# Causal scores in quadrants of 32 queries, and a re-ordered cross-attention stage, in a gated transformer layer on one core

## The chip, the cores and the metric

The kernel runs on one core of a Trainium2 chip. The metric is the device time of one launch in microseconds (us); lower is better. The engines are TensorE (PE, with its weight load PEld shown apart), VectorE (DVE), ScalarE (ACT), GpSimd (POOL) and SyncE (SP), which issues nearly all transfers.

## The reference

The input is 16 sequences of 64 tokens with 256 features. With `ln` for a layer norm and `rms` for an RMS norm, the layer computes:

```
x = x + tanh(g0) * cross(ln(x), ctx)      # reference groups tokens as 2 x 512 queries
x = x + tanh(g1) * ffn(ln(x))
cross: q = x Wq, k = ctx Wk, v = ctx Wv, 16 heads of 128; q, k = rms(q), rms(k) with gains
       softmax(q k^T / sqrt(128)) v, then Wo
ffn:   h = rms(x); causal self-attention over each sequence of 64, 16 heads of 128, then wo
       t = rms(x + attention); router softmax over 16 experts, top 6, weights renormalised
       out = x + attention + sum_e cw_e * down_e(silu(gate_e t) * up_e t) + shared expert
```

In `ffn` the scores of a key later than the query are masked out before the softmax. Everything is float32.

## The kernel before

**Stages.** The 1,024 tokens are two halves of 512. There are six stages in this order: `a` (cross-attention) for half 0 and half 1, `b` (self-attention) for each half, `m` (experts in 25 chunks of 128 hidden units) for each half. `a` and `b` work on pairs of heads: eight pairs a stage, 16 of each kind in all. Every engine's program is one list of calls for each pair or chunk (`cross_pair`, `self_pair`, `chunk`), and semaphores order the engines against each other. The order of calls within each function is written by hand, and an engine never overtakes in it.

**Large products.** Weights and tokens are split into a rounded part `_hi` and a rest `_lo`, and each large product is three float32r matmuls (`project` L538, `add_output` L565, `project_values` L651). DVE and ACT write the `_hi` parts, POOL the `_lo` parts (L1645). Scores, head values and norm sums are plain float32, of which each matmul leaves two records in the trace.

**A cross-attention pair.** For pair `u`, PE runs `norm_q` (L672), `scores` (L697), the value product of the pair before (`context_values`, L729), the next pair's keys 0, queries 0, keys 1, the output of the pair before for head 0, queries 1, the output for head 1, in half 0 `value_out` (L661), and last `norm_k` (L680), the key norm sums of the next pair. Keys 0 of the next pair go to `bank_s`, so they wait until DVE has read the scores from there (semaphore `raw`, L1365). `norm_q` waits until DVE has taken queries 0 from `bank_q` (`qt`, L1407), and `scores` until ACT has taken queries 1 (`qt_1`, L1005). `norm_k` writes `bank_p`. ACT takes keys 0 and squares them, takes keys 1 (L1010), takes the exponentials (L1046), and squares keys 1, queries 0 and queries 1 (L1002). DVE scales the scores, takes and subtracts the maximum, waits for the exponentials, normalises (L1389 to L1393), takes queries 0, transposes the weights (L1401), rounds the weights of the pair after next (L1419) and, in half 0, splits the value product (L1457, `vo_lo`).

**Pieces.** The norms of the next stage's tokens are cut into pieces and put beside pairs and chunks by `plan_of`, each with a pair number and a slot. On DVE in a cross pair slot 2 lies between the subtraction of the maximum and `normalise`, slot 0 in the middle, slot 1 at the end. A "turn" piece transposes tokens on PE into `bank_t` and `bank_p`; `norm_k` of that pair waits until DVE has read them (`release(held)`).

**A self-attention pair.** `scores` (L707) multiplies, for each head and sequence, 64 queries by 64 keys: 16 matmuls of 64 stationary columns and 64 moving ones, two sequences side by side. DVE multiplies by the scale and adds the mask, a row of 64 keys for each query (L1374). PE transposes the normalised weights (`turn_attn`, L714), ACT copies them to `rows_t` (`take_turned`), and `head_values` (L746) uses them.

**Passage to self-attention.** Beside the last cross pair, PE makes the first self-attention pair's queries 0, keys 0, both outputs, queries 1, the last context values, keys 1, values of the first tiles, values of the second tiles. Keys 0 and keys 1 both use `bank_k`; the context values of the last pair use `bank_v`, `bank_s`, `bank_p`, `bank_t`; both halves of the values use `bank_v`, and ACT empties it between them (L1022).

## Time and profile before

| what | value |
|---|---|
| median of 3 runs | 637.55 us (637.42 to 637.81) |
| profiled execution, own time | 637.76 us |
| its span, first to last instruction | 636.0 us |
| outside the span | 1.76 us |
| busy PE / DVE / ACT / POOL | 623.6 / 463.0 / 320.5 / 252.8 us |
| HBM read and written | 48.22 and 1.05 MB |

Busy time is the union of an engine's instructions. PE's instructions overlap each other, so a group's share of the order of work is told by its start and the start of what follows, not by the sum of durations.

### The profile page before, as it was taken

The numbers are of one execution on the slowest core, as the hardware profiler recorded it, in microseconds if no ns is written. First come the engines' busy times: TensorE is split into PE (matmuls) and PEld (weight loads), VectorE is DVE, ScalarE is ACT, GpSimd is POOL, SyncE is SP. The second block draws the span as 40 slices with busy tenths as digits, with TensorE's granted clock in tenths as the row PEclk, the third lists the DMA queues.
The fourth block names the chain that finished last, engine by engine and source line by source line (L and its number), as shares of the span: only waits on it lengthen the run. The fifth ranks groups of instructions, "written<-read, shape, count | busy, mean of one in ns | idle before, by whom it ended". The sixth has DMA issues, their size and how long they took to land.

```text
span 636.0 us, 17180 instructions
## 1 busy us (share of the span) xinstructions
PE 623.6 (98%) x6688; PEld 544.8 (86%) x6688; DVE 463.0 (73%) x913; ACT 320.5 (50%) x699; POOL 252.8 (40%) x336
## 2 busy tenths in 40 slices
PE   8899999999999999999999999999999999999997
PEld 6688888877788998999999998988888888888886
DVE  5878877998886776876677788655556987555556
ACT  6777767677743335333344333354476444444443
POOL 3221121212132533444352444445554665555453
PEclk9999999999999999999999999999999999999999
DMA  7523131111011322222221331113323232333332
GB/s 225 189 64 89 51 97 33 33 46 37 17 51 34 116 73 81 69 67 68 68 87 48 108 91 39 35 51 99 88 87 98 78 101 84 92 97 99 94 90 90
DMA packets 36019, 50.24 MB, mean 79 GB/s; under 512 B 4080, under 2 KB 23024, under 8 KB 35952
## 3 DMA queue, kind: packets, MB, share of 16 engines
q1 hardware_dynamic: 35376, 48.81, 26.1%
q8 instruction: 49, 0.80, 0.5%
q10 hardware_dynamic: 576, 0.48, 0.2%
q14 instruction: 18, 0.15, 0.1%
HBM read 48.22 MB, written 1.05 MB: 77 GB/s over the span
## 4 chain that ended last, share of the span: by engine, by line
PE 88%; DVE 5%; ACT 3%; issue 1%; DMA 1%; SPq 0%; POOL 0%; DVEq 0%; ACTq 0%
PE acc L565 23%; PE bank_q L538 16%; PE bank_k L538 14%; PE bank_s L538 7%; PE bank_v L538 7%; PE bank_v L651 7%; PE bank_s L707 3%; PE bank_p L746 2%; PE bank_s L697 2%; PE bank_k L729 2%; PE bank_t L714 1%; PE bank_k L661 1%; PE bank_p L680 1%; PE bank_q L672 1%; DMA xt<-in_ctx_t 1%
## 5 line engine op out<-in xcount | busy, mean ns | idle before, releaser
L565 PE MATMUL acc<-wo_hi,pv_hi 128*128 128x256 f32 x328 | 93.4, 285 | 0.3 <-DVE pv_lo L1482 0.2
L565 PE MATMUL acc<-wo_lo,pv_hi 128*128 128x256 f32 x328 | 92.9, 283 | 0.0
L565 PE MATMUL acc<-wo_hi,pv_lo 128*128 128x256 f32 x328 | 92.1, 281 | 0.0
L1645 POOL TENSOR_TENSOR wq_lo<-raw_a,wq_hi 128x256 fp32r<-128x256 f32 x32 | 23.6, 738 | 121.2 <-DVE wq_hi L1419 121.2
L565 PEld LDWEIGHTS acc<-wo_hi,pv_hi 128*128 128x128 f32 x328 | 61.5, 188 | 4.9 <-issue 1.8
L1645 POOL TENSOR_TENSOR wq_lo<-raw_m,wq_hi 128x256 fp32r<-128x256 f32 x50 | 40.4, 808 | 60.5 <-DVE wq_hi L1438 59.0
L565 PEld LDWEIGHTS acc<-wo_lo,pv_hi 128*128 128x128 f32 x328 | 61.7, 188 | 2.3
L565 PEld LDWEIGHTS acc<-wo_hi,pv_lo 128*128 128x128 f32 x328 | 62.3, 190 | 0.0
L1482 DVE TENSOR_TENSOR pv_lo<-raw_a,pv_hi 128x512 fp32r<-128x512 f32 (+1 forms) x51 | 37.9, 745 | 33.3 <-ACT pv_hi L1086 33.0
L538 PE MATMUL bank_q<-xt_hi,wq_hi 128*128 128x512 f32 x144 | 59.9, 416 | 0.5 <-POOL wq_lo L1645 0.5
L1086 ACT ACTIVATE pv_hi<-raw_a 128x512 fp32r<-128x512 f32 (+1 forms) x51 | 31.7, 624 | 56.5 <-DVE raw_a L1477 50.8
L1469 DVE TENSOR_TENSOR r_k<-ln_k,unit_w 128x512 f32<-128x512 f32 x44 | 32.0, 727 | 35.4 <-ACT ln_k L1077 35.4
L538 PE MATMUL bank_q<-xt_hi,wq_lo 128*128 128x512 f32 x144 | 56.7, 394 | 0.0
L538 PE MATMUL bank_q<-xt_lo,wq_hi 128*128 128x512 f32 x144 | 56.4, 392 | 0.0
L1645 POOL TENSOR_TENSOR wk_lo<-raw_m,wk_hi 128x256 fp32r<-128x256 f32 x50 | 39.3, 786 | 32.6 <-ACT wk_hi L1161 32.4
L1645 POOL TENSOR_TENSOR wv_lo<-raw_v,wv_hi 128x512 fp32r<-128x512 f32 x16 | 20.6, 1288 | 73.4 <-DVE wv_hi L1445 73.4
L1010 ACT ACTIVATE kt<-bank_k 128x512 f32<-128x512 f32 x48 | 28.7, 598 | 40.7 <-PE bank_k L538 40.6
L538 PE MATMUL bank_k<-xt_hi,wk_hi 128*128 128x512 f32 x114 | 44.9, 394 | 0.2 <-DVE pv_lo L1337 0.2
L538 PE MATMUL bank_k<-xt_lo,wk_hi 128*128 128x512 f32 x114 | 44.9, 394 | 0.0
L538 PE MATMUL bank_k<-xt_hi,wk_lo 128*128 128x512 f32 x114 | 44.6, 391 | 0.0
L1645 POOL TENSOR_TENSOR wq_lo<-raw_b,wq_hi 128x256 fp32r<-128x256 f32 x32 | 24.8, 777 | 48.6 <-DVE wq_hi L1422 48.6
L1645 POOL TENSOR_TENSOR wo_lo<-raw_m,wo_hi 128x256 fp32r<-128x256 f32 x50 | 41.3, 826 | 6.8 <-ACT wo_hi L1155 6.8
(235 smaller groups left out, 1951.6 us busy)
## 6 DMA issues: line engine op xcount, KB each, us to landing
raw_m<-in_chunk_m SPq DMA_DIRECT2D x50, 256.0 KB, 2.7
raw_a<-in_head_a SPq DMA_DIRECT2D x48, 192.0 KB, 3.1
raw_b<-in_head_b SPq DMA_DIRECT2D x32, 256.0 KB, 3.3
raw_m<-in_chunk_m SPq DMA_DIRECT2D x50, 128.0 KB, 2.1
raw_v<-in_pair_v SPq DMA_DIRECT2D x16, 256.0 KB, 3.1
raw_b<-in_head_b SPq DMA_DIRECT2D x32, 128.0 KB, 2.1
xs<-in_x SPq DMA_DIRECT2D x6, 128.0 KB, 3.3
out<-xs SPq DMA_DIRECT2D x3, 256.0 KB, 2.4
```

The lines of the kernel that those rows point to most:

```text
L538: last = nc.tensor.matmul(bank[:], w[:, cols], m(k), start=n == 0, stop=n == 3 * chunks - 1)
L565: last = nc.tensor.matmul(acc[t // 2][:, (t % 2) * D:(t % 2 + 1) * D], w[:, tok], m, start=begins and n == 0, stop=True, skip_group_check= ...
L651: last = nc.tensor.matmul(bank_v[:, b * PAIR:(b + 1) * PAIR], m, w[:, cols], start=n == 0, stop=n == 3 * KD - 1)
L697: last = nc.tensor.matmul(bank_s[j * GROUP:(j + 1) * GROUP, g * SEQ:(g + 1) * SEQ], qt[:, h, queries], kt[:, h, at:at + SEQ], start=True, ...
L707: last = nc.tensor.matmul(bank_s[s * SEQ:(s + 1) * SEQ, g * SEQ:(g + 1) * SEQ], qt[:, h, tok], kt[:, h, tok], start=True, stop=True)
L729: last = nc.tensor.matmul(context_of(u, j)[:, :, n, :], ctx_sb[rows, at:at + C], turned[rows, n, k], start=k == 0, stop=k == 1)
L746: last = nc.tensor.matmul(value_bank(r)[c * SEQ:(c + 1) * SEQ, cols], values[rows, n, width], turned[rows, cols], start=True, stop=True)
L1010: nc.scalar.activation(kt[:, h], bank[:], ACT.Copy).then_inc(stage["kt"], 1)
L1086: nc.scalar.activation(pv_hi[:, u.parity, part], hh[:, part], ACT.Copy).then_inc(M["hh_hi"], 1)
L1469: nc.vector.tensor_tensor(gu, gs, weights, ALU.mult).then_inc(M["weighted"], 1)
L1482: nc.vector.tensor_tensor(pv_lo[:, u.parity, part], hh[:, part], pv_hi[:, u.parity, part], ALU.subtract)\
L1645: nc.gpsimd.tensor_tensor(lo, raw, hi, ALU.subtract).then_inc(signal, 1)
```

## The change

The scores of self-attention are made in quadrants of 32 queries. `g` now stands for (part, head, parity of the sequence), where part 0 is queries 0 to 31 and part 1 is queries 32 to 63. Part 0 is multiplied by keys 0 to 31 alone, part 1 by all 64. That is 32 matmuls of 32 stationary columns, half with 32 and half with 64 moving columns. The quarter of the score tile that is left out is set to -1e30 once (`mask_rest`), and the scaling becomes two DVE instructions. The copy to `rows_t` and the moving operand of `head_values` follow the new order.

In cross-attention: the keys of the first two pairs change banks, so that the first pair need not wait for `raw` before keys 0; `norm_k` writes `bank_v` after a turn and always waits for `qt_1`; the wait for turned tokens moves to the next pair's context values; ACT squares queries 0 before it takes keys 1; DVE takes queries 0 before the slot 2 piece and `normalise`; the pieces `norm` (half 0), `refine` with `centre`, and `refine_root` with `apply` move to slot 2. In the passage to self-attention the first values go before the last context values, and keys 0 and 1 use `bank_s` and `bank_q`. In the expert stage `refine_root` and `apply` run before `split_hidden`.

```diff
-    beside_pairs("a", 0, ("x", 1), stats=(pairs - 5, 2), norm=(pairs - 4, 1), turn=(pairs - 3, 0))
-    beside_pairs("a", 1, ("y", 0), stats=(1, 2), rough=(1, 1), refine=(2, 2), centre=(2, 1), sums=(3, 0), root=(3, 1),
-                 refine_root=(4, 2), apply=(4, 1), turn=(5, 0))
+    beside_pairs("a", 0, ("x", 1), stats=(pairs - 5, 2), norm=(pairs - 4, 2), turn=(pairs - 3, 0))
+    beside_pairs("a", 1, ("y", 0), stats=(1, 2), rough=(1, 1), norm=(2, 2), sums=(3, 0), root=(3, 1), scale=(4, 2),
+                 turn=(5, 0))
...
-            return ((bank_k, bank_p, bank_t, bank_v) if u.deferred else (bank_v, bank_s, bank_p, bank_t))[j]
+            return (bank_k, bank_p, bank_t, bank_v if u.deferred else bank_s)[j]
...
-            return (bank_s, bank_k)[h] if u.kind == "a" else bank_k
+            if u.kind == "a":
+                return (bank_k, bank_s)[h] if u.n <= 2 else (bank_s, bank_k)[h]
+            return (bank_s, bank_q)[h] if u.very_first else bank_k
+        def key_sums(u):
+            turned = u.n > 1 and plan.piece(u.prev())[0] == "turn"
+            return (bank_v if turned else bank_p)[:, 0:HT // 2]
...
             def norm_k(u):
                 pe.wait_ge(A["sq_k"], u.of(1))
+                if not u.very_first:
+                    pe.wait_ge(A["qt_1"], u.n)
...
-                for h in range(2):
-                    for b in range(NS):
-                        t, s = b // SPB, b % SPB
-                        at = sequence_at(t, s) * SEQ
-                        tok = slice(at, at + SEQ)
-                        g = h * NT + t
-                        last = nc.tensor.matmul(bank_s[s * SEQ:(s + 1) * SEQ, g * SEQ:(g + 1) * SEQ], qt[:, h, tok],
-                                                kt[:, h, tok], start=True, stop=True)
+                for g in range(G):
+                    part, h, n = g // 4, g // 2 % 2, g % 2
+                    seen = (part + 1) * GROUP
+                    for j in range(QUADS):
+                        at = (2 * j + n) * SEQ
+                        queries = slice(at + part * GROUP, at + (part + 1) * GROUP)
+                        last = nc.tensor.matmul(bank_s[j * GROUP:(j + 1) * GROUP, g * SEQ:g * SEQ + seen], qt[:, h, queries],
+                                                kt[:, h, at:at + seen], start=True, stop=True)
...
             def cross_pair(u):          # PE
+                    release(turned_tokens(prev))
                     context_values(prev)
                 if nxt.kind == "a":
-                    pe.wait_ge(A["raw"], u.n)
+                    if prev:
+                        pe.wait_ge(A["raw"], u.n)
                     project_keys(nxt, 0)
...
-                if prev:
+                if nxt.kind == "b" or not prev:
+                    pe.wait_ge(A["raw"], u.n)
+                else:
                     pe.wait_ge(A["pv_lo"], QUADS * (prev.n - 1) + 1)
                 project_keys(nxt, int(nxt.kind == "a"))
...
                     project_queries(nxt, 1)
+                    project_values(nxt, False)
+                    pe.wait_ge(B["kt"], nxt.of(0))
                     context_values(u)
                     project_keys(nxt, 1)
-                    pe.wait_ge(A["pv_lo"], QUADS * (u.n - 1) + 2)
-                    project_values(nxt, False)
                     project_values(nxt, True)
+                    pe.wait_ge(A["pv_lo"], QUADS * u.n)
...
             def cross_pair(u):          # ACT
                     square_k(nxt, 0)
+                    square_q(nxt, 0)
                     take_k(nxt, 1)
                 exponentials(u)
                 if nxt.kind == "a":
                     square_k(nxt, 1)
-                    square_q(nxt, 0)
...
                 else:
+                    take_v(nxt, False)
                     take_context_values(u)
                     take_k(nxt, 1)
-                    take_v(nxt, False)
...
+            def mask_rest():
+                v.wait_ge(ld_rest, 16)
+                rest = by_part(sc[:])[:, 0, :, GROUP:SEQ]
+                mask = sm[:, SM_MASK:SM_MASK + GROUP].unsqueeze(1).to_broadcast([P, G // 2, GROUP])
+                link(nc.vector.tensor_scalar(rest, mask, 0.0, -1e30, ALU.mult, ALU.add))
...
-                    nc.vector.scalar_tensor_tensor(sc[:], found, SCALE, mask, ALU.mult, ALU.add).then_inc(B["scaled"], 1)
+                    for part in range(2):
+                        seen = (part + 1) * GROUP
+                        mask = sm[:, SM_MASK + SEQ - seen:SM_MASK + SEQ].unsqueeze(1).to_broadcast([P, G // 2, seen])
+                        scaled = nc.vector.scalar_tensor_tensor(by_part(sc[:])[:, part, :, 0:seen],
+                                                                by_part(found)[:, part, :, 0:seen], SCALE, mask,
+                                                                ALU.mult, ALU.add)
...
             def cross_pair(u):          # DVE
+                if nxt.kind == "a":
+                    take_q(nxt, 0)
                 prepare_piece(*piece_at(u, 2), u)
                 normalise(u)
-                if nxt.kind == "a":
-                    take_q(nxt, 0)
...
-                prepare_piece(*piece_at(u, 1), u)
...
-                with_scalar = piece_at(u)[0] in ("turn", "logits", "spread", "refine_root", "apply")
+                with_scalar = piece_at(u)[0] in ("turn", "logits", "spread")
```

## Rows read from the trace of the kernel before

**Rows 1.** The page: span, busy time by engine, granted clock in 40 slices.
```profile
span 636.0 us, 17180 instructions
...
PE 623.6 (98%) x6688; PEld 544.8 (86%) x6688; DVE 463.0 (73%) x913; ACT 320.5 (50%) x699; POOL 252.8 (40%) x336
...
PEclk9999999999999999999999999999999999999999
```

**Rows 2.** The page: the chain that ended last, by engine.
```profile
PE 88%; DVE 5%; ACT 3%; issue 1%; DMA 1%; SPq 0%; POOL 0%; DVEq 0%; ACTq 0%
```

**Rows 3.** PE's waits over the span: total, times, longest.
```profile
PE bank_s L538 <- DVE sc_sub L1365: 3.0, 4, 0.9
...
PE bank_q L672 <- DVE qt L1407: 0.8, 1, 0.8
PE bank_v L651 <- ACT vs L1022: 0.8, 1, 0.8
...
PE bank_k L729 <- issue: 0.6, 1, 0.6
PE bank_q L538 <- POOL wq_lo L1645: 0.5, 1, 0.5
PE bank_p L680 <- DVE xt_lo L1297: 0.5, 1, 0.5
...
PE bank_k L538 <- DVE pv_lo L1337: 0.2, 1, 0.2
```

**Rows 4.** Timeline, PE: one set each of small matmuls; start, duration.
```profile
208.68 1.15 PE L707 MATMUL bank_s<-kt,qt 128*64 128x64 f32 x32
...
169.29 1.10 PE L697 MATMUL bank_s<-kt,qt 128*32 128x64 f32 x64
...
358.20 0.74 PE L772 MATMUL bank_s<-sm,xt 128*32 128x16 f32 x64
```

**Rows 5.** Groups by form, PE: busy, mean ns of one, idle before.
```profile
L729 PE MATMUL bank_p<-rows_t,ctx_sb 32*128 32x128 f32 x128 | 18.5, 283 | 0.0
...
L714 PE MATMUL bank_t<-sm,attn 128*128 128x128 f32 x64 | 9.7, 274 | 0.0
```

**Rows 6.** PE's waits, 12 to 30 us.
```profile
PE bank_s L538 <- DVE sc_sub L1365: 1.4, 2, 0.9
```

**Rows 7.** Timeline, ACT, first pair.
```profile
21.23 0.59 ACT L1002 ACTIVATE sq_q<-bank_q 128x512 f32<-128x512 f32 x1
...
22.38 0.69 ACT L1005 ACTIVATE qt<-bank_v,gqk 128x512 f32<-128x512 f32 x1
```

**Rows 8.** Timeline, DVE and POOL, around the norm pieces.
```profile
6.05 1.13 DVE L1267 TENSOR_SCALAR hn<-xs,mv 128x256 f32<-128x256 f32 x4
...
67.22 2.51 DVE L1267 TENSOR_SCALAR hn<-xs,mv 128x256 f32<-128x256 f32 x4
...
133.91 2.53 DVE L1277 TENSOR_SCALAR ys<-xs,mv,st 128x256 f32<-128x256 f32 x4
...
133.87 0.73 POOL L1645 TENSOR_TENSOR wq_lo<-raw_a,wq_hi 128x256 fp32r<-128x256 f32 x1 [7.09 <-DVE wq_hi L1419]
...
141.88 0.69 DVE L1389 TENSOR_REDUCE ex_sum<-ex 128x8 f32<-128x512 f32 x1 [0.83 <-ACT ex L1046]
```

**Rows 9.** Timeline, ACT and PE: queries 1 taken in two pairs, one set of norm sums.
```profile
145.59 0.68 ACT L1005 ACTIVATE qt<-bank_v,gqk 128x512 f32<-128x512 f32 x1
...
167.08 0.68 ACT L1005 ACTIVATE qt<-bank_v,gqk 128x512 f32<-128x512 f32 x1
...
168.86 0.64 PE L672 MATMUL bank_q<-sq_q,ones_of 128*32 128x256 f32 x8
```

**Rows 10.** Timeline, DVE and POOL, the expert chunk with `refine_root`.
```profile
472.61 0.69 DVE L1482 TENSOR_TENSOR pv_lo<-raw_a,pv_hi 128x512 fp32r<-128x512 f32 x1 [0.76 <-ACT pv_hi L1086]
...
474.22 0.29 DVE L1438 CAST wq_hi<-raw_m 128x256 fp32r<-128x256 f32 x1
...
474.59 1.11 POOL L1645 TENSOR_TENSOR wq_lo<-raw_m,wq_hi 128x256 fp32r<-128x256 f32 x1 [2.06 <-DVE wq_hi L1438]
```

More of the change, by code:

```diff
@@ L627, in project_keys @@
                 pe.wait_ge(stage["wk_lo"], u.of(h))
-                if h and u.kind == "b":
+                if h and bank is bank_k and u.kind == "b":
                     pe.wait_ge(B["kt"], u.of(0))
+                if h and bank is bank_q:
+                    pe.wait_ge(B["qt"], u.of(1))
                 if u.kind == "a":
@@ L678, in norm_k @@
                 pe.wait_ge(A["sq_k"], u.of(1))
+                if not u.very_first:
+                    pe.wait_ge(A["qt_1"], u.n)
                 for j in range(QUADS):
-                    last = nc.tensor.matmul(bank_p[j * GROUP:(j + 1) * GROUP, 0:HT // 2], ones_of[:, 0:GROUP],
+                    last = nc.tensor.matmul(key_sums(u)[j * GROUP:(j + 1) * GROUP], ones_of[:, 0:GROUP],
                                             quads(sq_k[:])[:, :, :, j, :], start=True, stop=True)
@@ L736, in head_values @@
                 pe.wait_ge(B["attn_t"], u.n)
-                turned = rows_t[:].rearrange("p n h q -> p (n h q)")
+                turned = rows_t[:].rearrange("p n a q -> p (n a q)").rearrange("p (n a h q) -> p n h a q", a=2, h=2, q=GROUP)
                 values = vs[u.n % 2]
@@ L746, in head_values @@
                             last = nc.tensor.matmul(value_bank(r)[c * SEQ:(c + 1) * SEQ, cols], values[rows, n, width],
-                                                    turned[rows, cols], start=True, stop=True)
+                                                    turned[rows, n, h], start=True, stop=True)
                 last.then_inc(B["pv_done"], 1)
@@ L787, in prepare, with turned_tokens @@
                 return []
+            def turned_tokens(u):
+                piece, step = piece_at(u)
+                return [(xt_lo_ready, KD * (PREP[step] + 1))] if piece == "turn" else []
             def release(held):
@@ L822, in cross_pair @@
                     output(prev, 0)
-                held = prepare(u)
+                prepare(u)
                 if nxt.kind == "a":
@@ L1031, in log_k @@
                 act_e.wait_ge(A["ssk_done"], u.n)
-                nc.scalar.activation(half_wide[0], bank_p[:, 0:HT // 2], ACT.Ln, bias=eps5[:, 0:1]).then_inc(A["ln_k"], 1)
+                nc.scalar.activation(half_wide[0], key_sums(u), ACT.Ln, bias=eps5[:, 0:1]).then_inc(A["ln_k"], 1)
             def root_q(u):
@@ L1049, in take_turned @@
                 act_e.wait_ge(B["t_done"], u.n)
-                nc.scalar.activation(rows_t[:].rearrange("p n h q -> p (n h q)"), bank_t[:], ACT.Copy).then_inc(B["attn_t"], 1)
+                nc.scalar.activation(rows_t[:].rearrange("p n a (h q) -> p (a h) n q", q=GROUP),
+                                     bank_t[:].rearrange("p (b n q) -> p b n q", n=QUADS, q=GROUP), ACT.Copy)\
+                    .then_inc(B["attn_t"], 1)
             def take_context_values(u):
@@ L1271, in prepare_piece @@
                         last.then_inc(tok_ready, 1)
-                if piece in ("norm", "refine") and kind != "x":
+                if piece == "norm" and kind != "x":
                     await_root()
                     refined_root()
-                if piece in ("norm", "centre") and kind != "x":
                     for t in range(NT):
@@ L1372, in scale_scores @@
                 else:
-                    mask = sm[:, SM_MASK:SM_MASK + SEQ].unsqueeze(1).to_broadcast([P, G, SEQ])
-                    nc.vector.scalar_tensor_tensor(sc[:], found, SCALE, mask, ALU.mult, ALU.add).then_inc(B["scaled"], 1)
+                    for part in range(2):
[4 more added lines that the diff above has]
+                                                                ALU.mult, ALU.add)
+                    scaled.then_inc(B["scaled"], 1)
             def take_max(u):
@@ L1553, in self_pair @@
                 if u.very_first:
-                    v.wait_ge(ld_rest, 16)
+                    mask_rest()
                 scale_scores(u)
```

7 lines of the change are left out of this document (3 added, 4 removed).

## The prediction

> **What bounds the kernel now.** I read the page first. PE is busy for 623.6 of 636.0 us at the full granted clock in every slice, so its clock has nothing to give back [rows 1], and the chain that ended last runs through PE for 88% of the span [rows 2]. Each engine runs a fixed list, so only two things can shorten the time: less work on PE, or less idle time on it. Other engines matter where PE waits for them. So the second view is PE's waits. It has few entries, and those that the change touches are 3.0 us in four waits for the scaled scores (`raw`), 0.8 for queries 0 (`qt`), 0.8 for the values that ACT copies out of `bank_v`, 0.6 put down to "issue", 0.5 for `wq_lo`, 0.5 for turned tokens, and 0.2 for `pv_lo`: 6.4 us together [rows 3]. The third view is the timeline of PE for the small matmuls, because the change swaps one kind for another. The fourth is the timeline of DVE, ACT and POOL around each wait, to see what was late.
>
> **Part 1, the scores of self-attention.** Sixteen pairs each lose one set of L707. A set is 16 matmuls of 64 by 64 columns and takes 1.15 us [rows 4]. In its place come 32 matmuls of 32 stationary columns, half with 64 moving columns and half with 32. No row has this mixture, but two rows enclose it. The cross-attention set L697 is 32 matmuls of 32 by 64 columns in 1.10 us. The router's set L772 is 32 matmuls of 32 by 16 columns in 0.74 us [rows 4]. The wide half is therefore half of 1.10, or 0.55. The narrow half lies between half of 0.74 and half of 1.10. Cutting the moving columns from 64 to 16 saved only a third, so something beside the moving columns, most likely the 32 stationary ones, already sets the pace at 16. Were the pace of 64 columns moving alone, 32 of them would cost half of it, 0.28 for the narrow half, which is below what L772 shows. So I take L772's rate: 0.37. The new set is 0.55 + 0.37 = 0.92 us, and 16 x (1.15 - 0.92) = 3.7 us. The other end is a narrow half as dear as the wide one: 16 x (1.15 - 1.10) = 0.8 us.
>
> A rule speaks against the gain. The Trainium skill, TensorEngine Tiling (Array Packing), section Instruction Overhead, says that every matmul carries an overhead of about 60 cycles and that one moving column costs as much as 60. By it the narrow half would gain almost nothing and the sum would take 0.8 us here. The rows disagree in part, since 16 columns ran a third faster than 64 [rows 4].
>
> On DVE the scaling becomes two instructions over 384 columns a partition instead of one over 512; this saves a little work and adds one start. `mask_rest` runs once. ACT's copy to `rows_t` writes in runs of 32. All three lie beside PE's projections and outputs of the same pair, and no wait of PE in the self-attention stages has these as its releaser [rows 3]. I cost them at nothing. Without that cover they would cost some 0.2 us a pair, 3 us in all. `head_values` reads its moving operand in two runs of 32. L729 reads four such runs at 283 ns a record, L714 one run of the same 128 columns at 274 [rows 5]; so I take nothing, and 9 ns for each of the 1,024 records could not add up in sequence, since they overlap four deep: at most about 2 us.
>
> **Part 2, the first two pairs.** PE waits twice for `raw` here, 1.4 us, the longest 0.9 [rows 6], and 0.8 for `qt` [rows 3]. Keys 0 now go to `bank_k`, so the 0.9 goes. Taking queries 0 before the normalisation removes the 0.8. What is late next is ACT: `norm_k` must now wait until ACT has taken queries 1, and this began at 22.38 [rows 7]. ACT's chain before it starts up to 0.9 earlier, of which about 0.8 arrives past the exponentials, and the square of queries 0 (0.59, of which 0.5 until the next instruction starts) moves into ACT's wait for keys 1. So it begins 1.3 us earlier, near 21.1. With the two norm sets behind it, the second pair's scores come some 1.1 us earlier, and a little of the second `raw` wait goes too. I take 1.3 of the 2.2; the ends are 0.7 and 2.2.
>
> **Part 3, the norm pieces.** Four centring or scaling instructions take 2.51 and 2.53 us at the end of a pair, while the same four took 1.13 us at the start [rows 8]. The difference is POOL: at 133.87 it begins the low parts, right after the rounding, and so together with the piece at 133.91. Before that POOL had been idle for 7.09 us [rows 8]. In slot 2 the piece runs in this idle time, so it should cost about 1.13 and not 2.53: 1.4 us less. Besides, DVE waits 0.83 there for the exponentials in an ordinary pair [rows 8]. Taking queries 0 now fills most of that. So DVE reaches the next pair's norm sums at least 1.4 us earlier in each of the three pairs with a piece. The two late `raw` waits (3.0 - 1.4 = 1.6 us [rows 3, 6]) follow such pairs, and both are shorter than 1.4. The "issue" wait of 0.6 before L729 follows the piece of 67.22: the value product's split stands behind it on DVE, and the context values wait for it. I take 1.6 + 0.6 = 2.2 us. What is queued behind the piece in slot 2 is `normalise`, the transposed weights and the rounding for POOL. They become 1.7 us later, and PE needs them only in the next pair. The lower end is 1.0 us.
>
> **Part 4, the turn and the new wait.** `norm_k` after a turn goes to `bank_v`, so the 0.5 for turned tokens goes; queries 1 were taken at 167.08 + 0.68 = 167.76, before `norm_k` would want them [rows 9]. The wait for `qt_1` bites where ACT is late, in the pair with the four mean squares: there it was taken at 145.59 + 0.68 = 146.27. The moved square makes this 0.5 earlier, 145.75. Then come two norm sets of 0.43 each (168.86 to the scores at 169.29 [rows 4, 9]), so the scores start near 146.6. Before, only the scores waited for `qt_1`, and could start just after 146.3. That loses 0.2 to 0.3. Sum: 0.5 - 0.2 = 0.3 us.
>
> **Part 5, the passage to self-attention.** PE waited 0.8 for ACT to empty `bank_v` between the two value sets, and 0.2 for `pv_lo` [rows 3]. Now the last context values and keys 1 lie between the value sets, more than 2 us, and keys 0 have a bank of their own. The pipeline restarts behind each wait as well, so I take 1.2 for these 1.0 us of idle time. Late next could be the wait for `pv_lo` before the first scores; between it and the context values PE has keys 1 and the second values, over 2.5 us, against ACT's and DVE's 1.5. No loss.
>
> **Part 6, the expert stage.** DVE waits 0.76 for ACT before L1482 and then runs `refine_root`, so the rounding comes at 474.22, POOL begins at 474.59, and PE waits 0.5 [rows 3, 10]. Moved ahead of L1482, the five small instructions fill the 0.76. I take 0.5. `apply`, one chunk later, delays its L1482 by 1.1 to 2.5 [rows 8], which may cost up to 0.5 again; that is the lower end, 0.
>
> **Sum.** 3.7 + 1.3 + 2.2 + 0.3 + 1.2 + 0.5 = 9.2 us. Against the profiled execution's own 637.76 (span 636.0 and 1.76 around it) this gives 628.6. The median of the runs is 0.2 lower; I say 628.5.
>
> **The rivals.** (A) The forecast, 628.5: chance 0.60.
> (B) The narrow half saves nothing, since a short matmul takes as long as one of 64 columns: 637.6 - 0.8 - 5.5 = 631.3. For it: 16 columns still took two thirds. Against it: they took no more than that [rows 4]. Chance 0.14. This is what the Trainium skill's page TensorEngine Tiling (Array Packing), section Instruction Overhead, would have; the trace agrees with it only in that the cost does not fall in proportion.
> (C) The waits move instead of going: DVE's work is the same apart from POOL's part, so `raw` stays late, or the context values wait for the later weights. Half of the 5.5 us comes through: 637.6 - 3.7 - 2.7 = 631.2. For it: DVE had no idle time in the pairs with pieces. Against it: 1.13 against 2.53 [rows 8]. Chance 0.14.
> (D) B and C together: 637.6 - 0.8 - 2.7 = 634.1. Chance 0.05.
> (E) Slower: the wait for `qt_1` before `norm_k`. Two norm sets that ran ahead of it now stand behind it, 0.86 us, in up to 15 pairs, so 12.9 us at most, less 9.2: 641.2. It turns the sign once ACT takes queries 1 more than 0.6 us later than `norm_k` wants them in every pair. Against it: at 167.76 they were ready before. Chance 0.03.
> (F) Nothing measurable, gains lost to waits that I do not see: within 0.2%, 0.04.
>
> **Range.** 0.2% is 1.3 us, about what a measurement of this kernel can tell from no change. All of A to D are faster by more. Waits cost somewhat more than their idle time, so 11 us can come: 626.5. Upwards the range takes in B and C with an error of theirs, 632.5; it leaves out D, E and F. Faster 0.92, same 0.04, slower 0.04.
>
> **What would show it.** In the changed profile: a self-attention score set of 0.9 us, x64, in place of 1.15; distance between such sets shorter by 0.23; the norm pieces of four in about 1.1 us, before the sum of exponentials; no `raw` wait at the first pair and none after the piece pairs; no wait for `vs` in the passage; a short wait of L680 for `qt` near 146. A score set near 1.1 would show B. `raw` waits still there, or new waits of L729, would show C. Waits of L680 for L1005 in most pairs would show E.

## The result, and the profile after

The changed kernel takes 629.09 us (median of 4 runs, 628.85 to 629.23) against 637.53 (637.42 to 637.81) for the kernel before, a ratio of 0.9866 with a 95% interval of 0.9849 to 0.9884. The medians differ by 8.4 us. The profiled execution took 628.85, the shortest of the four, with a span of 627.1 in place of 636.0: 8.9 us less, and the table below is about these two executions. The forecast was 628.5 and case A.

The page after, its line of the span, of the engines, of the granted clock and of one queue:

```profile
span 627.1 us, 18234 instructions
PE 619.1 (99%) x7200; PEld 541.5 (86%) x7200; DVE 462.0 (74%) x930; ACT 320.5 (51%) x699; POOL 253.3 (40%) x336
PEclk9999999999999999999999999999999999999999
...
q8 instruction: 53, 0.87, 0.6%
```

PE is still the bound, at the full clock, which is the 2.4 GHz level in every slice [rows 1]. The waits of PE after (what is written, who releases it; us in total, times, longest):

```profile
PE bank_p L687 <- ACT qt L1021: 1.6, 2, 0.8
PE bank_s L932 <- POOL ones_of L1757: 1.5, 1, 1.5
PE bank_k L541 <- DVE ctxt_lo L1649: 0.5, 1, 0.5
PE bank_s L541 <- DVE sc_sub L1393: 0.2, 1, 0.2
PE acc L568 <- DVE pv_lo L1515: 0.2, 1, 0.2
PE bank_t L753 <- issue: 0.2, 1, 0.2
```

Of the 3.0 us for the scaled scores 0.2 is left. The waits for queries 0 (0.8), for the values (0.8), for `wq_lo`, for turned tokens and the "issue" before the context values are gone [rows 3]. So is the 0.2 for `pv_lo` before the keys. Two entries are new: 1.6 us in which `norm_k` (L687 now) waits for queries 1, and an "issue" inside the head values.

Where the time went is read from the starts of the score sets in both traces, which are marks of the same place in PE's list. "Won" is the difference of the starts, less the one at the mark before.

| stretch, up to | before | after | won | forecast |
|---|---|---|---|---|
| first pair's scores | 14.66 | 14.28 | 0.38 | none |
| third pair's | 35.60 | 33.80 | 1.42 | 1.3 (part 2) |
| seventh pair's (norm piece) | 81.47 | 78.98 | 0.69 | 0.6 of part 3 |
| half 1, sixth pair's | 156.66 | 153.68 | 0.49 | 0.5 to 0.6 (rest of part 3, less the new wait) |
| half 1, seventh pair's (turn) | 169.29 | 164.82 | 1.49 | 1.4 (rest of part 3, and 0.5 for the turn) |
| first self-attention scores | 195.78 | 189.89 | 1.41 | 1.2 (part 5) |
| first output of the experts | 412.75 | 404.21 | 2.64 | 3.7 (part 1) |
| the end | 635.98 | 627.05 | 0.39 | 0.5 (part 6) |

The forecast split part 3's 1.6 us only into "two waits"; the table gives 0.7 and 0.9 of it by their sizes [rows 3, 6].

### The profile page after: what moved, and what is told of

It reads as the page before. It is cut to its first block, busy times and chain, and to the rows that moved or that the text cites. A ratio compares the mean times of both kernels' runs of the same rounds, so it can differ in the third digit from the quotient of the medians.

```text
span 627.1 us, 18234 instructions
## 1 busy us (share of the span) xinstructions
PE 619.1 (99%) x7200; PEld 541.5 (86%) x7200; DVE 462.0 (74%) x930; ACT 320.5 (51%) x699; POOL 253.3 (40%) x336
## 3 DMA queue, kind: packets, MB, share of 16 engines
HBM read 48.22 MB, written 1.05 MB: 79 GB/s over the span
## 4 chain that ended last, share of the span: by engine, by line
PE 96%; DVE 1%; ACT 1%; DMA 1%; issue 1%; SPq 0%; DVEq 0%; ACTq 0%
PE acc L568 26%; PE bank_q L541 17%; PE bank_k L541 14%; PE bank_v L541 9%; PE bank_s L541 8%; PE bank_v L656 7%; PE bank_k L736 2%; PE bank_p L753 2%; PE bank_s L714 2%; PE bank_s L704 2%; PE bank_t L721 1%; PE bank_p L687 1%; PE bank_q L677 1%; PE bank_k L666 1%; DMA xt<-in_ctx_t 1%
## 5 line engine op out<-in xcount | busy, mean ns | idle before, releaser
L1515 DVE TENSOR_TENSOR pv_lo<-raw_a,pv_hi 128x512 fp32r<-128x512 f32 (+1 forms) x51 | 37.5, 737 | 31.8 <-ACT pv_hi L1104 31.5
L541 PE MATMUL bank_k<-xt_hi,wk_hi 128*128 128x512 f32 x110 | 43.1, 392 | 0.0
L541 PE MATMUL bank_k<-xt_lo,wk_hi 128*128 128x512 f32 x110 | 43.1, 392 | 0.0
L541 PE MATMUL bank_k<-xt_hi,wk_lo 128*128 128x512 f32 x110 | 43.1, 392 | 0.0
```

What stands on the lines that cost most here:

```text
L541: last = nc.tensor.matmul(bank[:], w[:, cols], m(k), start=n == 0, stop=n == 3 * chunks - 1)
L1515: nc.vector.tensor_tensor(pv_lo[:, u.parity, part], hh[:, part], pv_hi[:, u.parity, part], ALU.subtract)\
```

## The scores: experiments on part 1

The timeline of PE after, at the second self-attention pair: the set, and the first head value behind it. (A merged line of the timeline names the form of its first record only; the set holds both forms.) Below it the groups of L714 by form (count, then busy time and mean ns of one record):

```profile
202.58 0.95 PE L714 MATMUL bank_s<-kt,qt 128*32 128x32 f32 x64
203.46 0.27 PE L753 MATMUL bank_p<-rows_t,vs 64*64 64x64 f32 x1
```

```profile
L714 PE MATMUL bank_s<-kt,qt 128*32 128x64 f32 x512 | 10.8, 221 | 0.0
L714 PE MATMUL bank_s<-kt,qt 128*32 128x32 f32 x512 | 7.3, 199 | 0.0
```

The set takes 0.95 us, where 0.92 was forecast. Fourteen of the sixteen pairs are 0.20 us shorter (by the starts of the sets), not 0.23. One is 0.15 shorter, and one is longer by 0.31, for a reason that has its own section. Within a set four records begin every 56 ns in the wide half and every 32 ns in the narrow one. The router's set, of 16 moving columns, also shows four every 32 ns.

**The scores alone.** The kernel before, with the quadrants of `scores`, the scaling in two, `mask_rest` and the new order of `rows_t`; nothing in cross-attention. Of the edit only the loop is shown.

```diff
 def scores(u):
-    for h in range(2):
-        for b in range(NS):
-            ... bank_s[s * SEQ:(s + 1) * SEQ, g * SEQ:(g + 1) * SEQ], qt[:, h, tok], kt[:, h, tok]
+    for g in range(G):
+        part, h, n = g // 4, g // 2 % 2, g % 2
+        seen = (part + 1) * GROUP
+        for j in range(QUADS):
+            ... bank_s[j * GROUP:(j + 1) * GROUP, g * SEQ:g * SEQ + seen], qt[:, h, queries], kt[:, h, at:at + seen]
```

> The kernel before with the quadrant scores alone (new score loop, masks, scaling in two parts, copy and moving operand of the head values); cross-attention, the passage and the expert stage stay as before. My theory, that the parts add up: the 16 score sets give 0.20 us each, 3.2 us, so about 634.3 us, and the waits of before for the scaled scores, 3.0 us in four, stay. Rival 1, that the narrow tiles gain only together with a cross-attention stage that is no longer late: no change, 637.5. Rival 2, a wait in self-attention that the reordered weights or the two scaling instructions bring: over 635.

Measured: 634.96 us (634.81 to 635.89), ratio 0.9963 (0.9949 to 0.9976), span 633.2. In its timeline the set, and then its waits of PE, the groups that answer to [rows 3]:

```profile
208.20 0.95 PE L707 MATMUL bank_s<-kt,qt 128*32 128x32 f32 x64
```

```profile
PE bank_s L538 <- DVE sc_sub L1378: 3.0, 4, 0.9
...
PE bank_q L672 <- DVE qt L1425: 0.8, 1, 0.8
PE bank_v L651 <- ACT vs L1022: 0.8, 1, 0.8
PE bank_k L729 <- issue: 0.6, 1, 0.6
PE bank_t L746 <- issue: 0.5, 1, 0.5
```

Fourteen of the sixteen pairs are 0.20 to 0.22 us shorter, one is 0.15 shorter, and all waits of cross-attention that the change touches stay. Part 1 stands by itself and is about a third of the gain: 2.7 us by the medians. The 0.20 us a set that was expected is there, but one pair is 0.6 us longer than before. It has the one wait that is new, the "issue" at the head values (L746 here); a later section is about it.

**All 64 keys for both parts.** The changed kernel, with the masked quarter multiplied again.

```diff
-    ... bank_s[j * GROUP:(j + 1) * GROUP, g * SEQ:g * SEQ + seen], qt[:, h, queries], kt[:, h, at:at + seen]
+    ... bank_s[j * GROUP:(j + 1) * GROUP, g * SEQ:(g + 1) * SEQ], qt[:, h, queries], kt[:, h, at:at + SEQ]
```

> The changed kernel, but queries 0 to 31 are multiplied by all 64 keys in place of the first 32; the 32 matmuls and their 32 stationary columns stay, and the masked quarter is computed and not read. It tells the narrow moving operand from the quadrants. My theory: the set goes back to that of cross-attention, 1.10 us in place of 0.95, so 16 x 0.15 to 0.19 = 2.4 to 3.0 us slower than the changed kernel, about 631.8. Rival, that a matmul of 32 moving columns costs as much as one of 64: no difference, 629.1, and a set of 0.95 all the same.

Measured: 631.48 (630.88 to 632.21), ratio 0.9904 (0.9889 to 0.9919), span 630.0. Its set in the timeline:

```profile
202.62 1.10 PE L714 MATMUL bank_s<-kt,qt 128*32 128x64 f32 x64
```

Where nothing else is in the way, a pair is 0.13 to 0.15 us longer than with the narrow half, 2.2 us in sixteen, so rival B is refuted. The span is longer by 3.0 us; the rest are stalls of the kind just named, of which this execution had more. Of the 0.20 us a pair, 0.06 come from the quadrants themselves and 0.14 from the columns left out.

**16 keys for the first part.** Is there more to be had below 32 columns?

```diff
-    seen = (part + 1) * GROUP
+    seen = (16, SEQ)[part]
```

> The changed kernel, but queries 0 to 31 are multiplied by keys 0 to 15 alone; keys 16 to 31 of these queries keep what the bank held, so that part of the computation is left out. My theory, that at 32 moving columns the pace is already set by the 32 stationary ones, 32 ns for four records: no difference from the changed kernel, 629.1, set of 0.95 us. Rival, that the moving columns still count: half of 0.27 us a set less, 16 x 0.13 = 2.1 us, 627.0.

Measured: 629.61 (627.58 to 630.38), ratio 0.9865 (0.9849 to 0.9881), span 628.6.

```profile
202.37 0.94 PE L714 MATMUL bank_s<-kt,qt 128*32 128x16 f32 x64
```

The set is the same within 0.01 us, and no gain shows in the time (three stalls of the later section cost 0.5 to 1.1 us each in this execution). So at 32 moving columns the floor is already reached, as the forecast assumed when it took the router's rate for the narrow half. The Trainium skill, TensorEngine Tiling (Array Packing), section Instruction Overhead, puts one moving column on a level with 60. The measurement agrees that there is a floor but not with its height in columns: it lies at or above 32 and clearly below 64, since 64 cost 56 ns for four records and 32 and 16 both 32 ns. The four records stand side by side, one to a block of 32 stationary columns, so each of the four blocks takes a record every 32 ns, which at 2.4 GHz is 77 cycles. A record of 64 float32 columns takes 56 ns or 134 cycles, about two for a column. In cycles the floor is thus not far from the page's 60; in float32 columns it is reached at less than 40 (an estimate from these two rates).

## Cross-attention: experiments on parts 2 to 5

After, the pieces of the norms run in POOL's idle time. From the timeline of DVE and POOL:

```profile
61.82 1.13 DVE L1285 TENSOR_SCALAR hn<-xs,mv 128x256 f32<-128x256 f32 x4
...
128.40 1.38 DVE L1294 TENSOR_SCALAR ys<-xs,mv,st 128x256 f32<-128x256 f32 x4
...
150.34 1.14 DVE L1304 TENSOR_SCALAR hn<-ys,st 128x256 f32<-128x256 f32 x4
```

```profile
132.41 0.73 POOL L1677 TENSOR_TENSOR wq_lo<-raw_a,wq_hi 128x256 fp32r<-128x256 f32 x1 [7.64 <-DVE wq_hi L1452]
```

Two took 1.13 and 1.14, and the third 1.38, where 1.13 was forecast; before they took 2.51 and 2.53 [rows 8]. Why the third is longer is open: POOL was idle beside it too, as the 7.64 us before its next instruction show.

**The pieces back at the end of the pair**, with everything else as after: does taking queries 0 early cure the waits alone?

```diff
-    beside_pairs("a", 0, ("x", 1), stats=(pairs - 5, 2), norm=(pairs - 4, 2), turn=(pairs - 3, 0))
-    beside_pairs("a", 1, ("y", 0), stats=(1, 2), rough=(1, 1), norm=(2, 2), sums=(3, 0), root=(3, 1), scale=(4, 2),
-                 turn=(5, 0))
+    beside_pairs("a", 0, ("x", 1), stats=(pairs - 5, 2), norm=(pairs - 4, 1), turn=(pairs - 3, 0))
+    beside_pairs("a", 1, ("y", 0), stats=(1, 2), rough=(1, 1), refine=(2, 2), centre=(2, 1), sums=(3, 0), root=(3, 1),
+                 refine_root=(4, 2), apply=(4, 1), turn=(5, 0))
```

> The changed kernel, but the norm pieces of cross-attention stand at the end of the pair again (slot 1), where POOL makes its low parts. My theory: each set of four runs into POOL and takes 2.5 us in place of 1.1 to 1.4; the waits for the scaled scores after the two pieces of half 1 and the wait before the context values in half 0 come back in part. Taking queries 0 early still helps DVE by 0.6 us a pair, so of 0.6 + 0.7 + 0.9 us about 1.0 to 1.6 returns: 630.1 to 630.7. Rival, that early queries 0 alone cured these waits: 629.1 with sets of 2.5 us all the same.

Measured: 631.45 (630.76 to 633.6), ratio 0.991 (0.9897 to 0.9924), span 628.9. Its timeline of DVE and its first two waits of PE:

```profile
131.75 2.52 DVE L1295 TENSOR_SCALAR ys<-xs,mv,st 128x256 f32<-128x256 f32 x4
```

```profile
PE bank_s L541 <- DVE sc_sub L1394: 1.9, 3, 0.9
PE bank_p L687 <- ACT qt L1021: 1.8, 2, 0.9
```

The piece is at 2.52 us again, and there are three waits for the scaled scores in place of one: 1.9 us and not 0.2. The piece pairs lose 0.31, 0.54 and 1.03 us, 1.9 together, which is more than the 1.0 to 1.6 that were expected. So the place of the pieces is the cause, as part 3 said; early queries 0 alone do not cure these waits. The same instructions on the same data cost 1.13 to 1.38 us beside an idle POOL and 2.52 beside a busy one. The Trainium skill, SBUF — State Buffer, section Who interferes with whom, says that these two engines alone share a pair of ports, under an exclusive lock; the durations fit that, and no run here shows the lock itself.

**DVE takes queries 0 behind the normalisation**, as before.

```diff
 def cross_pair(u):          # DVE
-    if nxt.kind == "a":
-        take_q(nxt, 0)
 ...
+    if nxt.kind == "a":
+        take_q(nxt, 0)
```

> The changed kernel, but DVE takes queries 0 behind the normalisation again. My theory: only the first pair feels it, a wait of the query norm sums of up to 0.8 us, some of which hides in the wait for queries 1 that norm_k has there; in the pairs with pieces DVE gets 0.6 us later, and the shorter pieces still leave room: 0.2 to 0.8 us slower, about 629.6. Rival, that the piece pairs need the early queries as well: waits for the scaled scores come back near 134 and 156, 1 us or more slower.

Measured: 630.48 (630.22 to 630.89), ratio 0.9889 (0.9873 to 0.9904), span 628.4. The kernel is 1.4 us slower than the changed one, where 0.2 to 0.8 were expected, and the waits near 134 and 156 that the rival named are not there. The first pairs lose 0.46 us and those of half 1 0.39. The rest of the 1.4 us of span is a start-up later by 0.3 and a longer stall in the head values (0.25). Both differ as much between kernels that have the same code there, so they are taken as no work of the edit. So the early queries are worth some 0.9 us, the smaller partner of the pieces.

**The passage as before**: the values behind the last context values, keys 0 and 1 both in `bank_k`, and the banks of the last context values and ACT's order as before too (not shown).

```diff
-    return (bank_s, bank_q)[h] if u.very_first else bank_k
+    return bank_k
...
-    project_values(nxt, False)
-    pe.wait_ge(B["kt"], nxt.of(0))
     context_values(u)
     project_keys(nxt, 1)
+    pe.wait_ge(A["pv_lo"], QUADS * (u.n - 1) + 2)
+    project_values(nxt, False)
     project_values(nxt, True)
```

> The changed kernel, but the passage to self-attention has the order and banks of before. My theory: the waits for pv_lo and for the values return, 0.2 and 0.8 us of idle time, 1.4 us in the distance from the last cross-attention scores to the first of self-attention: 630.5. Rival, that these waits only absorbed time that is lost later anyway: 629.1.

Measured: 630.29 (629.75 to 630.54), ratio 0.9881 (0.9865 to 0.9896), span 628.7. The wait is back, and the passage is 1.27 us longer:

```profile
PE bank_v L654 <- ACT vs L1035: 0.8, 1, 0.8
```

Part 5's 1.2 is confirmed. The matmul that waits begins 1.05 us after the one before it, where its neighbours begin 0.11 apart: it costs 0.94 us for 0.78 of idle time. The other 0.3 lie on both sides of keys 0, where the view of PE's waits shows none. That fits part 5's reading that a wait costs PE more than its idle time.

**Free `norm_k` of the wait for queries 1.** The new wait stands where the forecast put it, in the pair of the four mean squares, and also in the first pair. From the timeline after, ACT and then PE:

```profile
20.58 0.69 ACT L1021 ACTIVATE qt<-bank_v,gqk 128x512 f32<-128x512 f32 x1
21.41 0.64 PE L687 MATMUL bank_p<-sq_k,ones_of 128*32 128x256 f32 x8 [0.84 <-ACT qt L1021]
...
141.78 0.68 ACT L1021 ACTIVATE qt<-bank_v,gqk 128x512 f32<-128x512 f32 x1
142.61 0.64 PE L687 MATMUL bank_p<-sq_k,ones_of 128*32 128x256 f32 x8 [0.79 <-ACT qt L1021]
```

PE begins `norm_k` 0.14 us after ACT has the queries, having idled 0.8. `norm_k` needs queries 1 out of the way only where it writes their bank, that is behind a turn:

```diff
 def norm_k(u):
-    if not u.very_first:
+    if u.n > 1 and plan.piece(u.prev())[0] == "turn":
         pe.wait_ge(A["qt_1"], u.n)
```

> The changed kernel, but norm_k waits for queries 1 only behind a turn, where it writes bank_v; elsewhere, in bank_p, it runs as early as before the change. My theory: the two waits of norm_k for queries 1 (1.6 us together) shrink to what the scores must wait anyway, and each place gives back up to two norm sets less what is needed for the squares, 0.4 to 0.8 us: 1.0 us faster than the changed kernel, about 628.1. Rival: the scores wait for the same semaphore a moment later, so nothing is won: 629.1.

Measured: 628.03 (627.64 to 628.46), ratio 0.9853 (0.9838 to 0.9868), span 625.8. The same kernel once more:

> The kernel with norm_k freed of the wait for queries 1, a second time, beside the one with the scores apart. Theory: 628.0 again, ratio 0.985; the third pair of half 1 gives 0.8 us against the changed kernel, the first pair nothing, since its context values wait for another engine. One or more stalls put down to issue near 245 or 317 us may show.

Measured: 628.26 (628.05 to 628.87), ratio 0.9856 (0.9841 to 0.9871), span 626.6. The waits of PE in the first of the two:

```profile
PE bank_s L541 <- DVE sc_sub L1393: 0.5, 1, 0.5
PE bank_k L736 <- ACT ln_k L1048: 0.5, 1, 0.5
PE bank_q L541 <- issue: 0.4, 1, 0.4
```

Both waits of `norm_k` are gone. The fifth pair of half 1 keeps what it wins, 0.84 and 0.87 us. The first pair wins 0.86 and loses 0.84 again in the second, where PE now waits for ACT and DVE instead: the wait only moved. So this wait costs 0.84 us in one place of the path, against a kernel without it. Both medians are below the changed kernel's 629.09 and the ratios 0.9853 and 0.9856 below 0.9866, but the intervals overlap, so a gain of about 0.9 us in the whole time is likely and not established. The 0.84 at the one place stands in both traces.

**The same, with the second half's context rounded in the third pair** instead of the first, to free DVE and ACT at the start. The edit stands in ACT's list and in POOL's.

```diff
-    if u.very_first:
+    if u.n == 3:
```

> The kernel with norm_k freed of the wait for queries 1 (but behind a turn), and in addition the rounding of the second half's context (ACT 0.6 us, POOL 1.3 us) moved from the first pair to the third. In the first pair it stood ahead of the key norm's logarithm, for which PE's context values waited 0.5 us, and POOL's part made DVE's scaling 1.5 us long. My theory: these 0.5 us and the 0.5 us behind them for the scaled scores mostly go: 0.6 to 1.0 us faster than with norm_k freed alone, 627.2. Rival, that the third pair pays the same: no difference, 628.0.

Measured: 629.11 (628.11 to 629.24), ratio 0.9864 (0.9847 to 0.988), span 627.3. The wait before the context values stays 0.5 and is now put down to another cause, and the stretch from the fourth pair's scores to the fifth's pays 0.32:

```profile
PE bank_s L541 <- DVE sc_sub L1393: 0.7, 2, 0.5
...
PE bank_k L736 <- issue: 0.5, 1, 0.5
```

The rounding was not what was late at the start, and that theory falls. What is late there stays open.

## The stalls in the head values

In the table, the experts' first output won 2.64 us, where sixteen pairs at 0.20 make 3.2. The difference is nearly all one place. From the timeline after:

```profile
246.13 0.27 PE L753 MATMUL bank_t<-rows_t,vs 64*64 64x64 f32 x1 [0.20 <-issue]
```

The start before it is 0.41 us earlier, in the middle of a run of matmuls with no semaphore between them, and that pair loses 0.5. The kernel before shows no such stall, in two traces. In ten of the twelve traces with quadrant scores PE stops so, one to three times each and fourteen times in all. From one start to the next it takes 0.4 to 1.3 us. The places are 204, 246 and 317 us of the span, 378 in the scores-only kernel and two others in the run below. Thirteen lie in the head values, one (with `norm_k` freed, at 246) in the projection of queries right behind them.

Counting PE's records (weight loads, matmuls and the sequencer's own) up to each stall gives 5825 at 204 us, 7105 at 246, 9153 at 317 and 10945 at 378, each within one. The distances, 1280, 2048 and 1792, are all multiples of 256. In the kernels with `norm_k` freed PE has 12 waits fewer ahead of these places. Their stalls still stand at the records 5825, 7105 and 9153, and so 12 weight loads or matmuls further on in the work.

The trace's instruction queue q8 moves packets of 16 KB. It went from 49 of them, in the page of the kernel before, to 53:

```profile
q8 instruction: 49, 0.80, 0.5%
```

The Trainium skill, Advanced Engine Details and Errata, section ISA Cache, says that a line of that cache is 16 KB or 256 instructions. It says that there are only two lines, but gives the size as 32 KB and as 128 KB on TensorE. The packets here are of that size and the stalls lie at that distance; how many lines PE has no run here shows.

The trace also has the time of each of these packets (the view of the DMA queues shows it when its window is made narrow). Numbered in order, the same packet goes with the same block of 256 records in every trace, up to the end of the self-attention stages. The 27th goes with the block that begins at 7105. Four of the stalls, and three blocks that begin without one:

| trace, block | its packet had landed | the block began | later by | stall |
|---|---|---|---|---|
| after, 7105 | 244.86 | 246.13 | 1.27 | 0.41 |
| 16 keys, 5825 | 202.92 | 204.34 | 1.42 | 0.47 |
| 16 keys, 7105 | 245.62 | 246.94 | 1.32 | 0.99 |
| scores alone, 10945 | 376.66 | 378.17 | 1.51 | 0.70 |
| after, 5825 | 198.01 | 204.05 | 6.0 | none |
| after, 9153 | 310.05 | 315.64 | 5.6 | none |
| before, 7105 | 257.81 | 266.43 | 8.6 | none |

All fourteen stalls end 1.27 to 1.51 us after their packet landed, and no block of any trace, up to 10945, begins less than 1.0 us after it. In the two traces of the kernel before no block of self-attention begins less than 4.9 us after it. So PE stops where the next 256 of its instructions have only just come.

A reason why it shows only now: scores and head values were 64 + 128 instructions of PE in 2.2 us and are 128 + 128 in 2.0. The packet of a block starts near the beginning of the block before it (between 3.1 us ahead and 3.8 us behind). A block of the self-attention stages lasted 6.5 us at least before, and the shortest lasts 2.5 now, the one that ends at 7105. That leaves little for a packet that takes 0.9 us or more and is wanted 1.3 us after it has landed. But the blocks that end at 5825 and 9153 last 5 us, and there PE stops only in the traces in which the packet starts late. Why it does in one trace and not in another stays open.

**PE's code shifted.** The changed kernel with 64 waits more in PE's program, all of them long met. The trace has 32 records for them, each of two waits, so the code behind lies 32 instructions later and not 64 as the expectation says.

```diff
+    for _ in range(64):
+        pe.wait_ge(setup_pool, SETUP)
```

> The changed kernel with 64 repeated waits, already met, in PE's program behind the warm-up, where PE is idle: the work is the same, the code behind lies 64 instructions later. It asks about the stalls of 0.4 to 1.0 us inside the head values (put down to issue, near 246 and 317 us in several traces) that no semaphore explains. My theory, that PE's code arrives late where 256 of its instructions run in 2 us: the stalls stand at other places or go, total time within 1 us of 629.1. Rival, that they come from data (a weight transfer in the way of PE's reads): they stay near 246 and 317 us.

Measured: 630.51 (630.23 to 632.11), ratio 0.9895 (0.9879 to 0.991), span 628.5. Its waits, and one of the stalls in its timeline:

```profile
PE bank_p L753 <- issue: 1.1, 1, 1.1
...
PE bank_t L753 <- issue: 0.2, 1, 0.2
```

```profile
387.98 0.21 PE L753 MATMUL bank_p<-rows_t,vs 64*64 64x64 f32 x1 [1.08 <-issue]
```

The stalls left 246 us and appear at 288.31 and 387.98, at records 8385 and 11457. These too are multiples of 256 away from the others (3072 from each other, 2560 from 5825), and PE goes on 1.40 and 1.42 us after the packet of the block had landed. The place hangs on where the code lies and not on data or on another engine.

**The kernel before once more**, for its own stalls; a single execution.

> The kernel before, unchanged, for a second trace of it. If stalls put down to issue inside the head values come only with the quadrant scores, this trace has none, like the first; if they come by chance to any of these kernels, it may have one. Time 637.5.

Measured: 637.53 us, span 635.7. Its waits of PE are those of [rows 3], with one of them 0.1 shorter and none at the head values:

```profile
PE bank_s L538 <- DVE sc_sub L1365: 3.0, 4, 0.9
...
PE bank_k L729 <- issue: 0.6, 1, 0.6
```

**Scores and head values apart.** `norm_k` is freed here as well. PE's order in a self-attention pair becomes head values, queries 0, scores, keys 0, to spread the dense code.

```diff
 def self_pair(u):          # PE
-    scores(u)
     head_values(prev)
+    pe.wait_ge(B["kt"], u.of(1))
+    pe.wait_ge(B["qt"], u.of(1))
     project_queries(nxt, 0)
+    scores(u)
```

> The kernel with norm_k freed, and in self-attention the order head values, queries 0, scores, keys 0 in place of scores, head values, queries 0, keys 0, so that the 128 and 128 small instructions of the two sets no longer follow each other. My theory, that PE's code arrives late where 256 instructions run in 2 us: the stalls put down to issue inside the head values go, and nothing else is late, since the scores come only 0.5 us later: 0 to 0.6 us faster than norm_k freed alone, whose own stalls differ from run to run, and a smaller spread. Rival, that the softmax chain now ends after turn_attn wants it: waits of L721 for attn in every pair, slower.

Measured: 671.36 (670.93 to 672.38), ratio 1.0528 (1.0514 to 1.0543), span 670.6. Its first wait of PE, its granted clock, and DVE's timeline in one pair:

```profile
PE acc L568 <- DVE pv_lo L1363: 24.9, 14, 1.8
```

```profile
PEclk9999999999998898898988998999999999999999
```

```profile
223.75 0.62 DVE L1407 SCALAR_TENSOR_TENSOR sc<-bank_s,sm 128x128 f32<-128x128 f32 x2 [4.65 <-PE bank_s L714]
```

The expectation was wrong; its rival named the softmax chain rightly, but the wait stands at the output product and not at L721. The scores come about 2.5 us later in the pair (head values 1.1, queries 0 1.4). DVE idles 4.65 us for them here, against 1.97 in the same pair after, and splits the head values only behind its work on the scores, so the output product waits 1.8 us in each pair. A pair in the middle lasts 16.0 or 17.5 us, against 13.8 after. The granted clock shows a lower digit in eight slices, all of them in the self-attention stages, and that is a second cost: two neighbouring pairs by `--windows`, with the granted clock as the last number but two:

```profile
222.76:240.28 17.52, 15.74 (x205) 13.80 (x205) 11.43 (x26) 4.89 (x10) 5.63 (x7) 0.90 0.21 60
240.28:256.31 16.03, 14.25 (x206) 12.31 (x205) 9.34 (x18) 6.91 (x18) 5.69 (x7) 1.00 0.22 68
```

The first had a stretch at 1.2 GHz, behind a wait of 1.8 us of PE, and took 1.5 us more with the same instructions. The second kept 2.4 GHz, with a wait of the same length. No stall of the kind above shows in this trace, but PE has so much idle time in every pair that the run does not say whether spreading the code took them away. It does say what the hand-written order is worth.

## Why the prediction was right, step by step

**Part 1** was right in kind and 0.5 us too high, then lost another 0.5. The term that was mis-sized is the set: 0.20 us a pair and not 0.23, 3.2 and not 3.7 us. The rate for the narrow half was right (four records every 32 ns, as in the router's set). Two halves of whole sets leave out the change of rate in the middle, where four records begin after 59 and 61 ns, and count the last record as half wide and half narrow, where it is a wide one. The stall was in no term. Two steps that were costed at nothing held: the second scaling instruction and the copy to `rows_t` release no wait, and `head_values` with its split operand does not slow down (a set and its head values together take 1.97 us and took 2.17, in every pair but the one with the stall).

**Part 2**: 1.42 for 1.3. The chain through ACT was read rightly: queries 1 were taken at 20.58, where the forecast had 21.1; of the 0.5 between them 0.38 is the earlier start of the whole trace.

**Parts 3 and 4** together gave 0.69 + 0.49 + 1.49 = 2.67 us, for 2.5. Part 4's wait was found where the forecast put it, but its price was told too low. The forecast's 0.2 to 0.3 is a net figure: the moved square brings ACT 0.5 forward, and two norm sets of 0.43 each then stand behind the wait. ACT had the queries at 142.46, `norm_k` began at 142.61, and the scores at 143.47. Without the wait the same place is 0.84 us shorter, as good as those two sets. So the change could have had 0.84 more there, which a net figure hides; and what it did have was a gain of 0.1 (PE was 2.82 us ahead of before at the scores ahead of this place and 2.95 at those behind it) and not a loss, since ACT's chain came earlier by more than 0.5: queries 1 were ready 3.8 us earlier in the trace, at 142.46 for 146.27 [rows 9], of which only 2.82 were won before. The turn and the pieces held their terms, the third piece with 1.38 us for 1.13.

**Part 5**: 1.41 for 1.2, of which the experiment gives 1.27 to the edit.

**Part 6**: 0.39 for 0.5. The timeline of DVE after shows the five small instructions ahead of L1515 (L1482 before), in the time in which it idled 0.76, and the rounding close behind:

```profile
463.22 0.16 DVE L1299 TENSOR_SCALAR st<-ms 128x4 f32<-128x4 f32 x1
463.41 0.59 DVE L1251 TENSOR_TENSOR st<-st 128x4 f32<-128x4 f32 x1
...
464.63 0.69 DVE L1515 TENSOR_TENSOR pv_lo<-raw_a,pv_hi 128x512 fp32r<-128x512 f32 x1
465.24 0.29 DVE L1471 CAST wq_hi<-raw_m 128x256 fp32r<-128x256 f32 x1
```

PE was 8.56 us ahead of before at this place, so the rounding (474.22 before) comes 0.4 earlier in the chunk, but L1515 (472.61 before) 0.6 later. The starts of PE's matmuls show both: its lead falls by 0.31 at the output that needs `pv_lo`, to 8.25, and rises by 0.70 behind it, where the wait for `wq_lo` had been. The forecast had the gain and not the loss. `apply`, one chunk later, took 2.08 us for 1.13 and cost PE nothing. All this is read from two traces; part 6 was tested in no run of its own.

**The first 0.38** is taken as no part of the change. The wait for the first context (`ctxt_lo`) is between nothing and 0.9 us long over these traces, and the first scores begin between 13.84 and 14.68; in the second trace of the kernel before they begin at 14.39 and not 14.66.

Of the rivals, B fell with the kernel of 64 keys, C in general with the pieces put back (their waits do not return while the pieces lie beside an idle POOL), and in particular holds for one wait, that of `norm_k`. E's place was right and its reach was not: two pairs and not fifteen. In rival E's sum a digit is off (637.6 + 12.9 - 9.2 is 641.3, not 641.2), and nothing hangs on it. The terms were right in kind, and that the total came within 0.6 us of the median is in part luck, because their errors lay on both sides: 0.5 and the stall's 0.5 too high in part 1, 0.1 in part 6, and 0.1 to 0.2 too low in part 2, in parts 3 and 4 together and in part 5, beside 0.38 at the start that belongs to none.

## What to carry over

Before a piece of work is moved on VectorE, look at what GpSimd does beside it: the same kind of four instructions cost 1.13 to 1.38 or 2.52 us by that alone. A wait put ahead of small work that used to run before it costs that whole work, even if the wait itself looks short. For small matmuls, find the floor from a row of the same stationary width (here 32 columns moved cost as little as 16), and cut no further.

## What was not expected of the hardware

PE stalled for 0.4 to 1.3 us with no semaphore involved, at distances of whole multiples of 256 instructions, in or right behind dense runs of small matmuls, and a shift of the code by 32 instructions moved the place. That it waits for its code is read from the traces, in which each stall ends 1.27 to 1.51 us after the packet with the next 256 instructions landed. It is not shown by an experiment: no run took the stalls away with the matmuls as dense as they are. In the trace of the kernel with the pieces put back none was seen, nor in that with scores and head values apart, and the other ten had one to three; this is likely behind part of the spread of 0.4 to 3 us between executions of one kernel. When a kernel gets twice as many instructions for the same columns, this is a cost that the sum of matmul times does not hold.
